# A transformer block on one core: the shared expert computed per 512-token chunk inside the span attention, with routed experts behind it

## The chip, the core and the metric

The kernel runs on one core of a Trainium2 chip. A core has five engines with instruction streams of their own: TensorE (PE: matmuls, with weight loads that overlap them), VectorE (DVE), ScalarE (ACT: activation functions from tables), GpSimd (POOL) and SyncE (SP, which issues most of the transfers). They meet only by semaphores. Matmuls write to eight banks of PSUM (128 partitions x 512 numbers each); everything else lies in SBUF. The metric is the device time of one execution in microseconds.

## What is computed

The reference takes x (32 sequences of 64 tokens, width 256, so 2048 tokens) and a context of 32 x 1601 rows, and applies three residual blocks. Cut to what matters:

```python
x = x + xattn(layernorm(x), ctx, ctx, mask, ...)   # 16 heads of 16, over 1601 keys
x = x + attn(layernorm(x), W_span, W_val, W_out)   # "span attention", below
x = x + ffn(layernorm(x), ...)

# attn: per head, scores depend only on a position and a learned mean and softness
span = head_reshape(h @ W_span.T, 2); value = head_reshape(h @ W_val.T, D)
mean = sigmoid(span[..., 0]) * m; soft = softplus(span[..., 1])
scores = -soft[..., None] * (pos - mean[..., None]) ** 2
out = softmax(scores) @ value; return reshape(out) @ W_out.T

# ffn: one shared expert for all tokens, two routed ones by a hash of the token's number
shared = silu(xf @ sw1 + sb1) * (xf @ sw3 + sb3) @ sw2 + sb2
for k in range(2):                                  # 8 experts, hidden width 256
    ids = (arange(N) * 11 + k * 7919) % 8
    out[tokens of e] += gelu(xs @ w1[e] + b1[e]) @ w2[e] + b2[e]
return (shared + out / 2) / 2
```

The hash depends on the token's number modulo 8 alone, so tokens fall into eight classes of 256, and each class has two experts. The shared expert is 256 to 512 (twice, one with Silu) to 256.

## The kernel before

The kernel works on transposed data: width on the partitions (two tiles, NK = 2), tokens along the columns. It has three phases. The first, cross attention (lines 455 to 842), takes nearly all of the span; the change doesn't touch it. The second and third are built by `tail` (line 845).

**Span attention** (`span_attention`, line 953) runs over four chunks of 512 tokens (eight sequences each). Its order is written out in the kernel, in three strings: `PE_ORDER`, `DVE_ORDER`, `ACT_ORDER`. A letter names a step and the digit its chunk; a repeated step counts its parts. `run_order` emits each engine's steps in that order, each with its semaphore waits. On TensorE: W the output projection of the cross attention, M and V the mean and the variance of the first layer norm (a matmul with a matrix of 1/256), S the span projection, T the transposition of its packed rows, A (eight per chunk) two matmuls that spread a pair of heads' factors, X (four per chunk) the value projections, U the sums of the exponentials, O their products with the values, Z the output projection, and m and v the second layer norm. On ScalarE: Q/q square, I/i inverse root (a logarithm and an exponential), S span activations, T copy of the transposed rows, B copy of a factor, E exponential of the distances, X value copies, L and U logarithm and exponential of the sums. On VectorE: W/Z add to x, C/c centre, N/n normalise, R pack, D distance (a product), O output, F the folding of the expert biases.
Banks 0 and 1 (`proj`) take W and Z, 2 and 3 (`ln_bank`) the layer norms, spans and turned rows, 4 to 7 factors, values, sums and products. All numbers in this part are 32-bit floats; most matmuls take them as two passes, while A and T use a one-pass format (F32R).

**Experts** (`expert_mlps`, line 1282) run after it, over the eight classes of 256 tokens. Every operand is split into a high and a low part in F32R, and `accumulate` (line 1465) makes three matmuls for each product: high-high, low part of the moving side, low part of the weights. Per class and in this order: the two hidden layers of the shared expert (48 matmuls), the first layers of both routed experts (24), and, one class late, the output (24 of the shared and 24 of the routed experts into one bank). ScalarE turns tokens into their high part, applies Silu and Gelu, and casts the results; the functions of the span attention, Silu and Gelu lie in different activation tables, and the program contains a table load at each switch. VectorE makes the low parts, gates, and adds class results to x in place. GpSimd splits the weights as they arrive through two buffers: six pieces early (sw1, sw3 and four first layers), the others once the last chunk's normalised tokens `h2` are complete. The last instruction on SP stores all of x, 2048 KB, after the last result.

Of the kernel before, what the change touches and what calls it, by code (L numbers as in the profile page):

```python
# [22 lines left out]
P = 128  # L23
# [821 lines left out]
def tail(nc, ins, bank, attn_out, out_done, wo, bo_all, mean_w, eps_col, ident, out_dram, sem):  # L845

    with ExitStack() as own:
        def sb(name, shape, dt=F32):
            return own.enter_context(nc.sbuf_tensor(name, shape, dt))

        x = sb("x", [P, NK, NTOK])
        h2 = sb("h2", [P, NK, NTOK])
        wval, wout = (sb(n, [P, NK, D]) for n in ("wval", "wout"))
        wspan = sb("wspan", [P, NK, 2 * H])
        sel_a, sel_b = sb("sel_a", [P, PAIRS, P], F32R), sb("sel_b", [P, PAIRS, P], F32R)
        head_ones = sb("head_ones", [P, 32])

        sw1, sw3 = ([sb(n + part, [P, NK, HS], F32R) for part in ("_hi", "_lo")] for n in ("sw1", "sw3"))
        w1 = [[sb(f"w1_{part}{i}", [P, NK, D], F32R) for part in ("hi", "lo")] for i in range(W_SLOTS)]
        weight = [sb(f"weight{i}", [P, NK * HS]) for i in range(2)]  # L860
        sb1, sb3 = sb("sb1", [P, HS // P]), sb("sb3", [P, HS // P])
        sb2, b1, b2 = sb("sb2", [P, NK]), sb("b1", [P, E, NK]), sb("b2", [P, E, NK])
        class_bias = sb("class_bias", [P, E, NK])
        bias_a, bias_b = sb("bias_a", [P, NK]), sb("bias_b", [P, NK])
        x_in = [sem(f"t_x_in{c}") for c in range(NCH)]
        w_in, sel_in, f_in, y_out = (sem("t_" + n) for n in ("w_in", "sel_in", "f_in", "y_out"))
        h2_done, f_done = sem("t_h2_done"), sem("t_f_done")

        def toks(c):
            return slice(c * CW, (c + 1) * CW)  # L870

        with nc.Block() as block:  # L872
            with ExitStack() as span:
                spans = span_attention(nc, span, bank, sem, mean_w, eps_col, ident, attn_out, out_done, x, h2, wo, bo_all, wspan, wval, wout,
                                       sel_a, sel_b, head_ones, x_in, w_in, sel_in, h2_done)
            mlps = expert_mlps(nc, own, bank, sem, ins, x, h2, weight, sw1, sw3, w1, sb1, sb3, b1, class_bias, f_in, h2_done, f_done, spans["first_rows"])

            @block.sync
            def _(sp):
                def load(tile, src, done):  # L880
                    sp.dma_start(tile, src).then_inc(done, 16)

                def rows(name):
                    return ins[name].rearrange("(k p) n -> p k n", p=P)

                for c in range(2):
                    load(x[:, :, toks(c)], rows("xT")[:, :, toks(c)], x_in[c])
                for name, tile in (("wspanT", wspan), ("wvalT", wval), ("woutT", wout)):
                    load(tile[:], rows(name), w_in)
                load(head_ones[:], ins["c_head_ones"], w_in)  # L890
                for c in range(2, NCH):
                    load(x[:, :, toks(c)], rows("xT")[:, :, toks(c)], x_in[c])
                for name, tile in (("sb1", sb1), ("sb3", sb3), ("sb2", sb2)):
                    load(tile[:], ins[name], f_in)
# [41 lines left out]
            @block.tensor  # L936
            def _(pe):
                spans["tensor"](pe)
                mlps["tensor"](pe)
# [651 lines left out]
```

## Time and profile before

| | us |
|---|---|
| median of 3 runs | 1577.74 |
| lowest, highest | 1574.93, 1578.54 |
| profiled execution | 1581.58 |
| its span | 1579.8 |
| TensorE busy | 1487.5 (94% of the span) |
| VectorE busy | 1002.9 (63%) |
| ScalarE busy | 917.8 (58%) |
| GpSimd busy | 424.8 (27%) |

A span is the profiled execution from its first to its last instruction. Busy time of TensorE includes a modelled way of each result through the array, so short groups of matmuls look longer than the gap to the next start. The granted clock (PEclk) is TensorE's clock as a share of 2.4 GHz; its other level is 1.2 GHz.

### The profile page before, as it was taken

What the parts mean: (1) busy time and instruction counts of PE and PEld (TensorE: products, weight loads), DVE (VectorE), ACT (ScalarE), POOL (GpSimd) and SP (SyncE); (2) the same over time, 40 slices, a digit from 0 to 9 for tenths busy, and PEclk for the clock granted to TensorE, in tenths of its full rate; (3) what the DMA queues carried; (4) which work ended last, traced back from release to release, by engine and by line L of the source; (5) the groups of instructions that cost most, each with busy time, mean ns of one, the idle gap of its engine ahead of it and who ended that gap; (6) DMA issues with size and microseconds to landing.
All of it is one profiled execution on the core that took longest, in us unless ns stands there. A gap on an engine that the chain in (4) does not pass through costs nothing. (4 is left out here: it accounts for less than half of the span.)

```text
span 1579.8 us, 56667 instructions
## 1 busy us (share of the span) xinstructions
PE 1487.5 (94%) x23708; PEld 1264.8 (80%) x23708; DVE 1002.9 (63%) x3974; ACT 917.8 (58%) x1836; POOL 424.8 (27%) x549
## 2 busy tenths in 40 slices
PE   6699999999999999999999999999999978886997
PEld 2578888888888888888888888888888844544997
DVE  4666677677666676767667667766666635442642
ACT  3346666665566665666556666665666644764653
POOL 0033333333333333333333333333333003002420
PEclk9899999999999999999999999999999998998999
DMA  5444444444444444444444444444444222000201
GB/s 150 139 121 109 109 109 109 109 109 109 112 119 121 127 113 106 117 112 121 110 116 114 116 113 117 116 110 110 109 109 109 68 86 85 2 1 8 61 21 54
DMA packets 89856, 156.28 MB, mean 99 GB/s; under 512 B 44784, under 2 KB 53744, under 8 KB 89328
## 3 DMA queue, kind: packets, MB, share of 16 engines
q1 hardware_dynamic: 89312, 151.56, 36.1%
q8 instruction: 191, 3.13, 0.9%
q0 software_dynamic: 288, 1.05, 0.2%
q14 instruction: 65, 0.53, 0.1%
HBM read 69.61 MB, written 4.19 MB: 47 GB/s over the span
## 5 line engine op out<-in xcount | busy, mean ns | idle before, releaser
L663 DVE CUSTOM_DVE_ANT_0 junk<-bank,mask_q 128x400 bf16<-128x400 f32 (+1 forms) x1024 | 546.9, 571 | 186.5 <-issue 180.3
L615 ACT ACTIVATE probs<-bank 128x512 f32<-128x512 f32 (+1 forms) x832 | 467.3, 595 | 123.2 <-PE bank L788 113.9
L591 POOL CAST ctx_hi<-ctx_raw 128x400 fp32r<-128x400 f32 x248 | 121.6, 519 | 847.8 <-PE bank L752 847.8
L788 PE MATMUL bank<-qstack,kstack 104*128 104x128 f16 (+1 forms) x3328 | 290.2, 220 | 4.2 <-ACT probs L615 3.4
L752 PE MATMUL bank<-wv_hi,ctx_hi 128*128 128x256 f32 (+1 forms) x832 | 280.1, 337 | 0.0
L769 PE MATMUL bank<-kstack,qstack 96*128 96x400 f16 (+1 forms) x1024 | 268.2, 336 | 7.4 <-issue 3.8
L654 DVE SCALAR_TENSOR_TENSOR k_lo<-bank,bk,k_hi 128x400 f16<-128x400 f32 (+1 forms) x256 | 162.2, 634 | 168.0 <-ACT k_hi L625 168.0
L635 ACT ACTIVATE v<-bank 128x256 f32<-128x256 f32 (+1 forms) x416 | 159.2, 383 | 188.5 <-PE bank L752 182.1
L788 PEld LDWEIGHTS bank<-qstack,kstack 104*128 104x128 f16 (+1 forms) x3328 | 214.2, 99 | 65.1 <-issue 16.7
L625 ACT ACTIVATE k_hi<-bank,bk 128x400 f16<-128x400 f32 (+1 forms) x256 | 152.1, 594 | 180.4 <-PE bank L742 172.3
L594 POOL TENSOR_TENSOR ctx_lo<-ctx_raw,ctx_hi 128x400 fp32r<-128x400 f32 x248 | 253.2, 1040 | 0.0
L752 PE MATMUL bank<-wv_lo,ctx_hi 128*128 128x256 f32 (+1 forms) x832 | 233.1, 280 | 0.0
L752 PE MATMUL bank<-wv_hi,ctx_lo 128*128 128x256 f32 (+1 forms) x832 | 232.7, 280 | 0.0
L803 PE MATMUL bank<-probs,v 128*32 128x64 f32 x13312 | 219.3, 220 | 8.1 <-issue 8.1
L803 PEld LDWEIGHTS bank<-probs,v 128*32 128x32 f32 x13312 | 197.4, 110 | 24.0 <-issue 16.4
L742 PE MATMUL bank<-ctx_hi,wk_hi 128*128 128x400 f32 (+1 forms) x512 | 190.4, 372 | 10.5 <-issue 9.7
L742 PE MATMUL bank<-ctx_lo,wk_hi 128*128 128x400 f32 (+1 forms) x512 | 177.4, 346 | 0.7 <-issue 0.7
L742 PE MATMUL bank<-ctx_hi,wk_lo 128*128 128x400 f32 (+1 forms) x512 | 178.0, 348 | 0.0
L752 PEld LDWEIGHTS bank<-wv_hi,ctx_hi 128*128 128x128 f32 (+1 forms) x832 | 154.7, 186 | 4.8
L752 PEld LDWEIGHTS bank<-wv_lo,ctx_hi 128*128 128x128 f32 (+1 forms) x832 | 154.9, 186 | 0.1
L752 PEld LDWEIGHTS bank<-wv_hi,ctx_lo 128*128 128x128 f32 (+1 forms) x832 | 153.3, 184 | 0.0
L769 PEld LDWEIGHTS bank<-kstack,qstack 96*128 96x128 f16 x1024 | 82.1, 98 | 55.7 <-issue 19.7
(169 smaller groups left out, 1727.2 us busy)
## 6 DMA issues: line engine op xcount, KB each, us to landing
ctx_raw<-in_ctxT SPq DMA_DIRECT2D x32, 1602.0 KB, 7.0
kstack<-k_hi SPq DMA_DIRECT2D x512, 100.1 KB, 2.2
kstack<-k_lo SPq DMA_DIRECT2D x256, 100.1 KB, 2.2
weight<-in_w SPq DMA_DIRECT2D x18, 256.0 KB, 2.7
x<-in_xT SPq DMA_DIRECT2D x8, 512.0 KB, 5.9
qstack<-q_parts SPq DMA_DIRECT2D x192, 16.0 KB, 5.6
out_yT<-x SPq DMA_DIRECT2D x1, 2048.0 KB, 6.4
weight<-in_sw SPq DMA_DIRECT2D x3, 512.0 KB, 6.6
```

Of the source, the lines that this page charges most:

```text
L591: nc.gpsimd.tensor_copy(c_hi[:, k, s0:s0 + n], raw[:, k, s0:s0 + n]).then_inc(ctx_hi, 1)
L594: nc.gpsimd.tensor_tensor(c_lo[:, k, s0:s0 + n], raw[:, k, s0:s0 + n], c_hi[:, k, s0:s0 + n].bitcast(F32), ALU.subtract).then_inc(ctx_lo, 1)
L615: nc.scalar.activation(probs[kt % NP][0:m, GROUPS * h:GROUPS * (h + 1), :], st[h][0:m, :], ACT.Exp, scale=DK ** -0.5 / (UP * UP)).then_inc ...
L625: nc.scalar.activation(k_hi[:, t, s0:s0 + n], pj[(b.slot + c) % 2][:, 0:n], ACT.Identity, bias=w["bk"][:, t:t + 1]).then_inc(khi_done, 1)
L635: nc.scalar.activation(heads, pj[(b.slot + NCK + i) % 2][0:m, 0:D].rearrange("s (p e d) -> s p e d", e=2, d=DK), ACT.Copy).then_inc(v_done, 1)
L654: nc.vector.scalar_tensor_tensor(k_lo[:, t, s0:s0 + n], pj[(b.slot + c) % 2][:, 0:n], w["bk"][:, t:t + 1], k_hi[:, t, s0:s0 + n], ALU.add, ...
L663: nc.vector.tensor_tensor_reduce(junk[i % SM][:, 0:n], sm[i % SM][:, 0:n], w["mask_q"][:, s0:s0 + n], 1.0, -3.0e38, ALU.add, ALU.max, part ...
L742: mm = nc.tensor.matmul(o, w[wp][:, k, t * P:(t + 1) * P], cp[:, k, s0:s0 + n], start=i == 0, stop=i == len(terms) - 1)
L752: mm = nc.tensor.matmul(o, cp[:, k, j * P:j * P + m], w[wp][:, k, :], start=i == 0, stop=i == len(terms) - 1)
L769: nc.tensor.matmul(sm[i % SM][:, 0:n], qstack[b.slot][0:KSTACK, p, :], kstack[b.slot][0:KSTACK, p, s0:s0 + n], start=True, stop=True).then ...
L788: mm = nc.tensor.matmul(st[h][0:m, g * PW:(g + 1) * PW], kstack[b.slot][0:KROWS, p, kt * P:kt * P + m], qstack[b.slot][0:KROWS, p, :], sta ...
L803: mm = nc.tensor.matmul(ob[32 * g:32 * g + 32, t * S:(t + 1) * S], v[b.slot][0:m, kt, c0:c0 + 2 * DK], probs[kt % NP][0:m, p, S * e:S * (e ...
```

## The change

`span_attention`, `expert_mlps` and the old `tail` become one function, `tail`, with one set of order strings. The shared expert leaves the classes. After a chunk's second layer norm, its tokens are split (H on ScalarE, h on VectorE) and laid out by class in `tokens`, which now holds all 2048; the normalised tokens are written over `xc[1]` and `h2` is gone. The shared expert then works on the 512 tokens of that chunk: F, in four parts (12 matmuls of 512 columns each, into banks 0 and 1; Silu F, gate F, cast G and remainder G behind it), and G, its output (24 matmuls), added to x by VectorE's step r. sw2 is scaled by 0.5 and the sum added directly, where it was scaled by 2 and the joint bank by 0.25. `proj_free` makes each user of banks 0 and 1 wait for all users ahead of it. F and G of chunks 0 to 2 stand between the steps of the span attention of the following chunk, those of chunk 3 between the first routed experts.
The routed experts keep their classes: K, first layers (24 matmuls of 256 columns, in banks 4 and 5 or 6 and 7 by turns), and P, second layers (24, in banks 2 and 3 by turns). Results go to eight tiles `y`, and SP stores each class in a transfer of 256 KB; all of its loads are issued ahead of the first store. The early pieces on GpSimd are now seven: sw1, sw3, sw2 and four first layers, which lie beside the span attention's buffers, while the slots of the second layers reuse them. The exponentials lie in the space of `attn_out`, and the output of the span attention overwrites `rs`. ScalarE's return to the logarithm and exponential table is written as a load by name.

```diff
-    PE_ORDER = """W0 M0 W1 V0 W2 S0 W3 T0 A0 M1 A0 A0 A0 A0 V1 A0 A0 S1 A0 T1 X0 U0 X0 M2 A1 X0 X0 V2 O0 S2 A1 Z0 A1 T2 A1 M3 m0 A1 A1
-        V3 A1 v0 A1 X1 X1 U1 X1 X1 A2 S3 O1 T3 A2 Z1 A2 A2 m1 A2 A2 A2 A2 v1 X2 X2 U2 X2 X2 A3 O2 A3 Z2 A3 A3 m2 A3 A3 A3 A3
-        v2 X3 X3 U3 X3 X3 O3 Z3 m3 v3"""
+    PE_ORDER = """W0 M0 W1 V0 W2 S0 W3 T0 A0 M1 A0 A0 A0 A0 V1 A0 A0 S1 A0 T1 X0 U0 X0 M2 A1 X0 X0 V2 O0 S2 A1 Z0 A1 T2 A1 m0 A1 M3 A1
+        v0 A1 V3 A1 X1 U1 X1 F0 A2 X1 X1 F0 S3 O1 F0 A2 A2 T3 Z1 A2 A2 F0 A2 m1 A2 A2 v1 G0 U2 X2 F1 A3 X2 X2 F1 X2 F1 O2 F1
+        A3 A3 Z2 A3 A3 m2 A3 G1 A3 v2 A3 X3 X3 U3 X3 F2 X3 F2 O3 F2 Z3 m3 F2 v3 G2 K0 F3 K1 F3 K2 F3 P0 F3 K3 P1 K4 G3 K5 K6
+        P2 P3 P4 K7 P5 P6 P7"""
...
+            def log_exp():
+
+                if table[0] != "log_exp":
+                    nc.scalar.preload_act_table_set("natural_log_exp_and_others")
+                table[0] = "log_exp"
...
+            def silu(c, m):
+                n = FT * c + m
+                table[0] = "silu"
+                act.wait_ge(s["f1"], n + 1)
+                if c == 0 and m == 0:
+                    act.wait_ge(s["f_in"], 5 * 16)
+
+                need(act, s["gate_lo_done"], n - 1)
+                nc.scalar.activation(gate[m % 2][:], proj[0][:, :], ACT.Silu, bias=sb1[:, m:m + 1]).then_inc(s["silu_done"], 1)
...
+            def proj_free(m):
+
+                need(pe, s["x1_done"], NK * emitted["W"])
+                need(pe, s["x2_done"], NK * emitted["Z"])
+                need(pe, s["silu_done"] if m == 0 else s["gate_done"], emitted["F"])
+                need(pe, s["shared_done"], NK * emitted["G"])
...
+            def shared_hidden(c, m):
+                pe.wait_ge(s["tok_lo_done"], c + 1)
+                pe.wait_ge(s["w_lo_done"], pieces.index("sw3") + 1)
+                for j, (weights, done) in enumerate(((sw1, s["f1"]), (sw3, s["f3"]))):
+                    proj_free(j)
+                    out = proj[j][:, :].rearrange("p (e t) -> p e t", e=E)
+                    accumulate(out, [(columns(weights, k, m), [chunk_tokens(part, k, c) for part in range(2)])
+                                     for k in range(NK)]).then_inc(done, 1)
+                emitted["F"] += 1
+
+            def shared_output(c, _):
+                pe.wait_ge(s["w_lo_done"], pieces.index("sw2") + 1)
+                pe.wait_ge(s["gate_lo_done"], FT * (c + 1))
+                for m in range(NK):
+                    proj_free(m)
+                    accumulate(proj[m][:, :], [(columns(sw2, k, m), [part[:, k, :] for part in gate_parts])
+                                               for k in range(FT)]).then_inc(s["shared"], 1)
+                emitted["G"] += 1
...
+            def store(n):
+                sp.wait_ge(s["f_done"], NK * (n + 1))
+                dst = out_dram.rearrange("(k p) (e t) -> p k e t", p=P, e=E)[:, :, order[n], :]
+                sp.dma_start(dst, y[n][:]).then_inc(y_out, 16)
```

How the instructions stand on the engines that the prediction walks through. TensorE at the turn from chunk 1 to chunk 2, before; from the top the value projections (L1251), the sums (L1259), a pair A (L1240, L1241), the spans of chunk 3 (L1213), products (L1268), transposition (L1222) and output projection (L1177):

```order
L1251 MATMUL bank<-wval,t_h 128x256 x4
L1259 MATMUL bank<-ex,head_ones 32x512 x8
L1251 MATMUL bank<-wval,t_h 128x256 x4
L1240 MATMUL bank<-rows,sel_a 128x512
L1241 MATMUL bank<-rows,sel_b 128x512
L1213 MATMUL bank<-wspan,t_h 128x32 x8
L1268 MATMUL bank<-ex,vbd 32x64 x64
```

The same place now; L1470 is the helper of the three-pass matmuls, L1445 the value projections, L1453 the sums (the exponentials lie in attn_out), L1434 and L1435 a pair A:

```order
L1445 MATMUL bank<-wval,t_h 128x256 x2
L1453 MATMUL bank<-attn_out,head_ones 32x512 x8
L1445 MATMUL bank<-wval,t_h 128x256 x2
L1470 MATMUL bank<-tokens_hi,sw_hi 128x512
L1470 MATMUL bank<-tokens_lo,sw_hi 128x512
L1470 MATMUL bank<-tokens_hi,sw_lo 128x512
...
L1434 MATMUL bank<-rows,sel_a 128x512
L1435 MATMUL bank<-rows,sel_b 128x512
L1445 MATMUL bank<-wval,t_h 128x256 x4
L1470 MATMUL bank<-tokens_hi,sw_hi 128x512
```

Two parts of F0, twelve matmuls each, stand among the value projections, and only one value projection stands ahead of the sums where two did.

ScalarE at the same place, before: an exponential, value copies (L1069), logarithm and exponential of the sums (L1078, L1083), a factor copy (L1050), and the span activations (L1032 and behind it):

```order
L1059 ACTIVATE ex<-dist 128x512
L1069 ACTIVATE vbd<-bank 64x8x16 x8
L1078 ACTIVATE rs<-bank 128x512 x2
L1069 ACTIVATE vbd<-bank 64x8x16 x4
L1083 ACTIVATE rs<-rs 128x1024
L1069 ACTIVATE vbd<-bank 64x8x16 x4
L1050 ACTIVATE b_copy<-bank 128x512
L1032 ACTIVATE e<-bank 128x64
```

And now, from the token cast (L1165) over the value copies (L1143), Silu (L1176) and gate cast (L1182) to the return of the table (L1079) ahead of the span activations:

```order
L1165 ACTIVATE tokens_hi<-t_xc 128x8x64 x2
L1143 ACTIVATE vbd<-bank 64x8x16 x4
L1153 ACTIVATE rs<-bank 128x512 x2
L1143 ACTIVATE vbd<-bank 64x8x16 x4
L1159 ACTIVATE rs<-rs 128x1024
L1176 ACT_TABLE_LOAD
L1176 ACTIVATE gate<-bank,sb 128x512
L1120 ACTIVATE b_copy<-bank 128x512
L1143 ACTIVATE vbd<-bank 64x8x16 x4
L1182 ACTIVATE gate_hi<-gate 128x512
L1143 ACTIVATE vbd<-bank 64x8x16 x4
L1176 ACTIVATE gate<-bank,sb 128x512
```

Token cast, Silu, gate cast and the switches of tables are new among the span attention's copies and exponentials.

## Rows read from the trace of the kernel before

**Rows 1.** The page's first line: the span and its instructions.

```profile
span 1579.8 us, 56667 instructions
```

**Rows 2.** Windows: start:end, length, then busy us of each engine, PEclk, DMA.

```profile
1372.20:1454.30 82.10, 60.55 (x580) 34.74 (x581) 31.69 (x56) 48.37 (x111) 1.79 (x1) 0.93 0.00 1
1454.30:1572.60 118.30, 116.87 (x960) 116.50 (x960) 55.25 (x94) 63.92 (x108) 34.02 (x31) 0.99 0.10 30
...
1374.10:1400.90 26.80, 23.26 (x213) 14.54 (x212) 13.89 (x28) 18.95 (x44) 0.00 (x0) 0.94 0.01 2
1400.90:1425.70 24.80, 19.33 (x196) 10.91 (x195) 10.19 (x17) 17.36 (x38) 0.00 (x0) 1.00 0.00 1
1425.70:1454.30 28.60, 16.06 (x169) 7.86 (x169) 6.72 (x12) 10.20 (x26) 1.79 (x1) 0.87 0.00 1
```

**Rows 3.** Chain that ended last: start us, length us, engine and line.

```profile
1452.45 0.73 ACT tokens_hi L1380 x2
...
1453.21 0.97 DVE tokens_lo L1419 x2
...
1454.31 110.90 PE bank L1465 x912
...
1566.14 5.99 PE bank L1465 x48
...
1572.16 0.42 DVE x L1441
```

**Rows 4.** Timeline of TensorE: start, length, form, count, [idle before <-releaser].

```profile
1365.65 0.40 PE L1240 MATMUL bank<-rows,sel_a 128*128 128x512 f32 x1
1365.88 0.39 PE L1241 MATMUL bank<-rows,sel_b 128*128 128x512 f32 x1
...
1374.13 1.92 PE L1259 MATMUL bank<-ex,head_ones 128*32 128x512 f32 x16
...
1400.95 1.93 PE L1259 MATMUL bank<-ex,head_ones 128*32 128x512 f32 x16
...
1407.46 1.99 PE L1268 MATMUL bank<-ex,vbd 128*32 128x64 f32 x128 [2.20 <-ACT vbd L1069]
...
1411.48 3.60 PE L1177 MATMUL bank<-o,wout 128*128 128x512 f32 x8
...
1421.59 1.88 PE L1204 MATMUL bank<-t_sq,mean_w 128*128 128x512 f32 x4
...
1425.68 1.92 PE L1259 MATMUL bank<-ex,head_ones 128*32 128x512 f32 x16
1427.54 1.99 PE L1251 MATMUL bank<-wval,t_h 128*128 128x256 f32 x8
...
1436.26 5.63 PE L1177 MATMUL bank<-o,wout 128*128 128x512 f32 x8 [1.44 <-DVE o L1161]
```

**Rows 5.** Groups by line, 1372.2 to 1454.3: busy us, mean ns of one, idle before.

```profile
L1153 DVE TENSOR_TENSOR dist<-bank,b_copy 128x512 f32<-128x512 f32 x16 | 10.6, 686 | 14.5 <-ACT b_copy L1050 12.7 <-ACT ex L1059 1.8
...
L1050 ACT ACTIVATE b_copy<-bank 128x512 f32<-128x512 f32 x16 | 9.1, 596 | 7.3 <-PE bank L1241 7.3
```

**Rows 6.** Timeline of ScalarE in the expert stage, as rows 4.

```profile
1468.61 1.28 ACT L1392 ACT_TABLE_LOAD   x1
1469.91 1.57 ACT L1392 ACTIVATE gate<-bank,sb 128x256 f32<-128x256 f32 x4
```

**Rows 7.** Groups by line on GpSimd, 1290 to 1580, as rows 5.

```profile
L1370 POOL TENSOR_TENSOR w_lo<-weight,w_hi 128x512 fp32r<-128x512 f32 x18 | 24.8, 1378 | 1.4
L1367 POOL CAST w_hi<-weight 128x512 fp32r<-128x512 f32 x18 | 13.0, 723 | 50.9 <-PE bank L1465 47.4 <-DMA weight<-in_w 3.4
...
L1364 POOL TENSOR_SCALAR weight<-weight 128x1024 f32<-128x1024 f32 x1 | 2.8, 2779 | 118.7 <-DVE h L1126 118.7
```

**Rows 8.** DMA issues of the page: KB each, median us from issue to landing.

```profile
weight<-in_w SPq DMA_DIRECT2D x18, 256.0 KB, 2.7
...
out_yT<-x SPq DMA_DIRECT2D x1, 2048.0 KB, 6.4
```

More of the change, by code:

```diff
@@ L963, in span_attention @@
     BLOCKS = CW // P
-    xc = [sb(f"t_xc{i}", [P, NK, CW]) for i in range(2)]
-    sq = [sb(f"t_sq{i}", [P, NK, CW]) for i in range(2)]
-    rstd = [sb(f"t_rstd{i}", [P, CW]) for i in range(2)]
-    h = [sb(f"t_h{i}", [P, NK, CW]) for i in range(2)]
-    e0, lnx, near, gap = (sb(n, [P, BLOCKS, H]) for n in ("e0", "lnx", "near", "gap"))
-    sg = sb("soft_gap", [P, BLOCKS, 2 * H])
-    packed = sb("packed", [P, BLOCKS, P], F32R)
-    ident_r = sb("ident_r", [P, P], F32R)
-    rows = [sb(f"rows{i}", [P, CW], F32R) for i in range(2)]
@@ L1308, in expert_mlps @@
+    assert max(i for i, step in enumerate(PE_ORDER.split()) if step[0] == "W") < min(PE_ORDER.split().index(step) for step in ("Z0", "F0"))
     order, arrival = [0], list(CLASS_EXPERTS[0])
@@ L1520, in expert_mlps @@
-    return {"sync": sync, "gpsimd": gpsimd, "scalar": scalar, "vector": vector, "tensor": tensor}
+    pieces += [("w1", i) for i in range(W_SLOTS)]
+    NEARLY = len(pieces)
+    pieces += [("w2", 0), ("w2", 1)] + [(w, i + lag) for i in range(E + 1 - W_SLOTS) for w, lag in (("w2", 2), ("w1", W_SLOTS))]
+    pieces += [("w2", i) for i in range(E + 3 - W_SLOTS, E + 1)]
+    names = ("x1_proj x1_done x2_proj x2_done span e0_done lnx_abs lnx_exp lnx_done vec packed_zero vbd_zero turn_ready packed_done turned "
+             "rows_done ab_ready b_copied dist_done ex_done sums lns_done rs_done val_ready vbd_done pv o2_done h_done h2_done "
+             "tok_hi_done tok_lo_done f1 f3 silu_done gate_done gate_hi_done gate_lo_done shared shared_done fe gelu_done gelu_hi_done "
+             "gelu_lo_done xb_done f_out f_done w_halved w_hi_done w_lo_done w_in sel_in f_in").split()
@@ new lines, in tail @@
+    s = {n: sem("t_" + n) for n in names}
+    x_in = [sem(f"t_x_in{c}") for c in range(NCH)]
+    weight_in = [sem(f"t_weight_in{i}") for i in range(2)]
+    y_out = sem("t_y_out")
+    mean, xc_done, sq_done, var, lnv, rstd_done = ([sem(f"t_{n}{i}") for i in range(2)]
+                                                   for n in ("mean", "xc", "sq", "var", "lnv", "rstd"))
+    norm_done = [s["h_done"], s["h2_done"]]
+    src_done = [s["x1_done"], s["x2_done"]]
+    bias_steps = sem("t_bias_steps")
```

973 lines of the change are left out of this document (478 added, 495 removed).

## Prediction

> **What bounds the kernel now.** I read the windows first, because an average over the whole span mixes stages. The attention over the context ends near 1291 us and the diff leaves it alone. Behind it lie the span attention (to 1454.3) and the expert stage. In the expert stage TensorE is busy 116.87 of 118.3 us; before it, from 1372.2 to 1454.3, 60.55 of 82.1 us, at a mean clock of 0.93, with ScalarE at 48.37 and VectorE at 31.69 [rows 2]. The chain of waits says the same: its last long piece is 110.90 us of matmuls on line 1465, then 5.99 us more, one result of 0.42 us, and the store [rows 3]. So the second stage is bound by TensorE's work, and the first by waits among three engines, in which TensorE stands still. Work carried from the second into the holes of the first can be had for less than its length. The question is how full the holes get.
>
> The first stage repeats per chunk. I take the matmuls of "sums" (the sums of the exponentials, line 1259) as milestones: U1 starts at 1374.13, U2 at 1400.95, U3 at 1425.68 [rows 4]. The last piece, U3 to the first expert matmul at 1454.31, is a bare dependency chain: 16.06 us busy of 28.6 [rows 2, 3].
>
> **Prices.** An expert matmul of 256 columns: 912 of them in 110.90 us [rows 3], 0.1216 each; with the first ones at half clock out of it 0.120. One of 512 columns in the same number format: two start 0.23 apart [rows 4], and that pair also changes its weights; twice 0.107 of streaming is 0.213. I take 0.22, within 0.213 and 0.23. The shared expert has 24 x 3 = 72 such matmuls per chunk: F, four pieces of 12 (2.6 us each, 10.5 together), and G, 24 (5.3). That is 15.8 per chunk, 63.4 in all; as 576 narrow ones it cost 69.1. The routed experts stay: 384 x 0.12 = 46.1.
> ScalarE gains per chunk four Silus, four casts and two token casts of 512 columns, near 0.60 each by the b_copy row [rows 5] (two token casts of half the width take 0.73 [rows 3]), so 6.0. A table switch occupies 1.28 [rows 6]. The order of the new kernel has 6 switches with chunk 0's pieces, 4 with chunk 1's, 2 with chunk 2's and 9 in the routed stage, 21 behind the first against 16 before. VectorE gains four gates, four remainders, two token remainders and two additions, 12 x 0.69 [rows 5] = 8.2 us per chunk; the class-permuted ones are bounded by 0.69 and by 0.97, the two narrow remainders of [rows 3]. It was busy 10.19 of 24.8 in the second cycle [rows 2]; VectorE does not bind.
>
> **Floors per cycle.** Second cycle: TensorE 19.33 busy at full clock [rows 2] plus 15.8 is 35.1. ScalarE 17.36 plus 6.0 plus 4 x 1.28 is 28.5. First cycle, ScalarE: 18.95 + 6.0 + 6 x 1.28 = 32.6. So TensorE remains the bound, with ScalarE close behind, and a new cycle cannot take less than about 35 where the old took 24.8 or 26.8.
>
> **Walking the new order.** I followed the three orders by hand, each step starting when its engine is free and what it reads is there, with these prices: on TensorE an averaging or variance step 1.8, an output projection 3.5, X 0.97, U 1.9, O 2.0, a pair A 0.46 (all issue time, by [rows 4], where the printed length holds also the last matmul's way through the array); on ScalarE 0.55 to 0.60 for 512 columns; on VectorE 0.69, 1.3 for a pair.
> U1: variance v0 now stands ahead of V3, so the last distance of chunk 1 comes earlier; U1 at 1372.3, 1.8 early (between 0 and 2). The first F waits for the token remainder until 1375.2.
> U1 to U2: U1 ends at 1374.2, X follows, F runs from 1375.2 to 1377.8. Its first half lets ScalarE begin at 1376.5, but there stand two groups of value copies, the sums' logarithm and their exponential; so the switch is at 1377.7, the Silu 1379.0 to 1379.6, the gate ends 1380.4. TensorE has A and two X until 1380.2: the second F waits for nothing. S, O and the third F end at 1389.3. T3 needs the packed rows, which VectorE makes from 1388.1 on, behind O1's outputs: 1390.7. Z1 runs 1391.3 to 1394.9; the last F waits for Z1's addition (1396.4) and ends at 1399.0; m1 at 1399.5; v1 waits for the square, which stands behind a Silu, a cast and two copies (1404.1); G0 1406.0 to 1411.2; U2 at 1411.2. TensorE's work in it is 35.6, so 3.3 idle.
> U2 to U3: Z2 waits for the switch and the fourth Silu (1431.2), G1 runs 1438.5 to 1443.7 over the squares, X3 waits for the last distance (1448.0); U3 at 1450.0, 36.1 of work and 2.7 idle.
> U3 to the routed experts: F2 pieces wait for Silu, switch and gate; Z3 at 1465.6, m3 1470.6, v3 1475.0, G2 1477.7 to 1482.9 over the inverse root, switch, normalisation, cast and remainder of chunk 3; routed experts at 1483.6, with 28.5 of work and 5.1 idle.
> Sum: 1372.3 + 100.2 work + 11.1 idle = 1483.6. Of the 100.2, 3 x 15.8 = 47.4 is carried in; the old kernel took 80.2 for the other 53 and stood or ran slowly for 27. So 47 us of work come in and the stage ends 29.3 later: 18 hidden.
> From there TensorE has 46.1 of routed work and 15.8 of chunk 3's shared work, 61.9. It should not wait: banks are double and results alternate; ScalarE has 9 switches (11.5), four Silus, four casts and the first three classes' activations against about 35 us up to the last G. The weight splits that now come behind the phase are 14, at 0.72 + 1.38 = 2.1 [rows 7], 29 in all; the first output needs two (4.2) and starts 16 us in. They hide; uncovered, the first two would cost 4.2. Doubling sw2 took 2.8 on GpSimd [rows 7]; its halving moves into the idle time before 1372, at nothing, since the first G is at 1406. The eight bias additions of x, now behind chunk 3's shared addition, cost VectorE some 5 us before the third result while TensorE has 2.8 per class: 0 to 2, I take 0.5. End of matmuls 1483.6 + 61.9 + 0.5 = 1546.0.
> **The end.** Result 0.4. The old store took from 1572.58 to 1579.8, 7.2, of it 6.4 landing for 2048 KB; a 256 KB load lands in 2.7 [rows 3, 8]. With the same 0.8 around it the last of eight stores takes 3.5, bounds 2.7 (nothing around it) and 7.2. That makes 1549.9.
> **Clock.** In the old stage Z3 took 5.63 against 3.60 for Z2, behind a wait of 1.44 [rows 4]; the granted clock of that cycle was 0.87 against 1.00 in the one before [rows 2], so part of it at 1.2 GHz. The walk has full clock. The new holes are shorter; I add 2, between 0 and 5 (what the old run lost). Span 1552; minus 27.8 against 1579.8 [rows 1]. The profiled execution took 1581.58, 1.8 above its span, and the median of the runs is 1577.74, so the change goes off that: **1549.9**.
>
> **Rivals.**
> *Holes filled wholly.* Neither idle nor slow clock: 1372.3 + 100.2 + about 3, then 61.9 and 3.9: 1541 span, 1539 predicted. For it: an order that keeps independent work at every wait. Against: F needs both output banks, which the residual path also uses.
> *Nothing hidden.* The waits stay as long and the shared work adds itself: 1372.3 + 53 + 27 + 47.4 + 61.9 + 3.9 = 1565.5, so 1563.4. Still faster, by narrow matmuls made wide (5.7), the smaller last store (3.7), and the early U1, wait and slow clock at the old seam. For it: ScalarE at 32.6 of the first cycle's 38.9, and each of 12 switches can stand ahead of an exponential for which X waits.
> *Switches dearer than their rows.* In the old trace a switch follows the cast at once and the next activation starts 1.30 behind it [rows 6]. If instead each cost its 1.28 once more on the path, the 12 of the span stage would add 15.4 to the span of 1552 (1565 predicted), and all 21 would add 26.9 (1577). The Trainium skill, ScalarE: Activation LUTs, section "What ACT_TABLE_LOAD costs", gives 1283 ns for the load and 1380 ns of drain, 2.66 us a switch. By that rule the 12 add 16.6 and the 21 add 29, so 1566.5 and 1579; the trace agrees with its 1283 but shows no second part.
> *Slower: pieces run one behind another.* F writes the two banks that Z writes. If every piece ran alone (2.6 matmul, 1.28 switch, 0.60 Silu, 0.69 gate = 5.2, four of them, then cast, remainder, 5.3, addition and switch back, 9.3) a chunk would cost 30, three 90: experts at 1372.3 + 80.2 + 90 = 1542.5, span 1608, predicted 1606. It decides from 20.5 us a chunk, against 15.8 of matmul. Against it: between F pieces stand A, X, S and O, which use other banks.
> *It doesn't do what it says:* the routed stage waits for weights. Fourteen splits each with its load unhidden, 2.1 + 2.7 = 4.8, are 67 against 61.9: 5 more, 1555; inside the forecast's range.
>
> **Chances.** Forecast (1543 to 1557) 0.60; filled wholly 0.13; nothing hidden or a part of the dearer switches (1557 to 1570) 0.19; dearer switches in full, about no change, 0.02; slower 0.06. A measurement can tell 0.2% from no change, some 3 us. Faster 0.92, same 0.02, slower 0.06. The range takes half of the outer two cases and the bounds of clock and store: 1538 to 1567.
>
> **What would show it.** In the profile after: U2 near 1411, U3 near 1450, first routed matmul near 1484 (right within 5); F matmuls 0.22 apart; TensorE waits in the routed stage under 2 us; switches 1.28; last store about 3.5. TensorE waiting for Silus or distances over 20 us between 1372 and the routed start would make the walk wrong; a routed stretch over 66 would make its hidden switches or weights wrong; a routed start later than 1514 would make it slower.

## The result, and the profile after

The changed kernel takes 1549.88 us (median of 4 runs, 1546.79 to 1550.99) against 1577.34 for the kernel before (4 runs, 1574.93 to 1578.54): 27.5 us less, ratio 0.9825, interval 0.9806 to 0.9844. The profiled execution took 1546.79 with a span of 1545.0.

The span is 34.8 us shorter than that of before, but not all of this is the change. The output projection W0, the first matmuls that the diff touches, starts at 1284.47 where it started at 1292.25: 7.8 us lie in the attention ahead of it, which is the same code; in the profiles of the variants below, with this same attention, it starts anywhere from 1281.2 to 1291.1. From W0 to the end of the span it is 260.5 us, where it was 287.5. That is 27.0 less, close to the difference of the medians. The steps are therefore compared below by their distance from W0.

Windows of the changed kernel: start:end, length, busy us of each engine, PEclk (the granted clock), DMA share, GB/s. The cuts are W0, the milestones U1, U2 and U3, the first routed matmul, and the last one's end.

```profile
core 0: us, PE busy (x) PEld busy (x) DVE busy (x) ACT busy (x) POOL busy (x), PEclk, DMA share, GB/s
1284.50:1363.40 78.90, 66.65 (x337) 36.37 (x337) 46.55 (x94) 40.82 (x83) 21.80 (x17) 0.88 0.28 88
1363.40:1403.10 39.70, 37.37 (x283) 26.10 (x282) 21.72 (x40) 33.32 (x61) 0.00 (x0) 1.00 0.00 1
1403.10:1443.20 40.10, 37.56 (x273) 25.91 (x272) 18.24 (x28) 28.76 (x53) 0.00 (x0) 1.00 0.01 2
1443.20:1478.30 35.10, 30.57 (x241) 19.75 (x240) 13.34 (x20) 19.16 (x35) 0.00 (x0) 1.00 0.00 1
1478.30:1541.70 63.40, 62.90 (x458) 59.13 (x456) 33.44 (x60) 37.17 (x65) 30.42 (x28) 1.00 0.26 80
```

These rows answer to [rows 2]. The two cycles grew from 26.8 and 24.7 to 39.7 and 40.1, and in them TensorE is now busy 94% of the time, at full clock, where it was busy 23.26 of 26.8 and 19.33 of 24.8. The stage of expert matmuls shrank from 118.3 to 63.4. The whole path from U1 (1363.39) to the first routed matmul (1478.45) is 115.1; before it was 80.2 to the first expert matmul, so 34.9 longer, for 216 matmuls of the shared expert carried in.

What still stops TensorE between 1362 and the end, from its waits (line waited, releaser, us in total, times, longest):

```profile
PE bank L1445 <- DVE dist L1291: 3.1, 2, 1.7
PE bank L1392 <- DVE x L1243: 1.8, 2, 1.4
PE bank L1363 <- DVE gate L1311: 1.7, 2, 1.0
PE bank L1434 <- DVE dist L1291: 1.5, 1, 1.5
PE bank L1470 <- ACT gate L1176: 1.3, 1, 1.3
PE bank L1470 <- issue: 1.2, 2, 0.8
PE bank L1470 <- DVE x L1243: 0.7, 1, 0.7
```

In all 11.3 us. Of the first line, 1.7 stands just ahead of U1, so 9.6 lie between U1 and the end: 2.9 for distances, 3.0 for gates and a Silu, 2.5 for additions to x, and 1.2 that the view puts down to no engine. The end of the chain that ended last, which answers to [rows 3] (start, length, what):

```profile
1471.89 0.82 issue
1472.71 53.92 PE bank L1470 x360
1526.63 0.39 issue
1527.02 14.59 PE bank L1470 x120
1541.63 0.42 DVE y L1344
1542.06 0.33 DVEq L1529
```

From 1472.71 TensorE runs its 480 last matmuls with one stop of 0.39: no weight, Silu or Gelu is waited for. From the last result (1542.06) to the end of the span is 2.9 us.

### The profile page after: what moved, and what is told of

Its sections match the earlier page's. It is cut to its first block and busy times, and to the rows that moved or that the text cites. A ratio compares the mean times of both kernels' runs of the same rounds, so it can differ in the third digit from the quotient of the medians.

```text
span 1545.0 us, 56243 instructions
## 1 busy us (share of the span) xinstructions
PE 1473.8 (95%) x23420; PEld 1243.0 (80%) x23420; DVE 1007.9 (65%) x3974; ACT 926.2 (60%) x1833; POOL 426.2 (28%) x549
## 3 DMA queue, kind: packets, MB, share of 16 engines
q0 software_dynamic: 288, 1.05, 0.2%
```

## The experiments

Times are medians; "before" is the kernel before on the same chip. Only the edit against the changed kernel is shown.

### The shared expert behind the span attention, in the new and in the old order

`e1_shared_behind` takes F and G of chunks 0 to 2, with their casts, gates and additions, out of the three strings and sets them behind the span attention.

```diff
...
-        v0 A1 V3 A1 X1 U1 X1 F0 A2 X1 X1 F0 S3 O1 F0 A2 A2 T3 Z1 A2 A2 F0 A2 m1 A2 A2 v1 G0 U2 X2 F1 A3 X2 X2 F1 X2 F1 O2 F1
-        A3 A3 Z2 A3 A3 m2 A3 G1 A3 v2 A3 X3 X3 U3 X3 F2 X3 F2 O3 F2 Z3 m3 F2 v3 G2 K0 F3 K1 F3 K2 F3 P0 F3 K3 P1 K4 G3 K5 K6
+        v0 A1 V3 A1 X1 U1 X1 A2 X1 X1 S3 O1 A2 A2 T3 Z1 A2 A2 A2 m1 A2 A2 v1 U2 X2 A3 X2 X2 X2 O2 A3 A3 Z2 A3 A3 m2 A3 A3 v2
+        A3 X3 X3 U3 X3 X3 O3 Z3 m3 v3 F0 F0 F0 F0 G0 F1 F1 F1 F1 G1 F2 F2 F2 F2 G2 K0 F3 K1 F3 K2 F3 P0 F3 K3 P1 K4 G3 K5 K6
...
```

> The changed kernel with F, G and r of chunks 0 to 2 moved out of the span attention, to between its last step and the first routed expert (11 table loads in place of 22). Theory, that the shared work fills holes of the span attention: 47 us of TensorE work no longer hidden, against 11 us of idle that stay in the changed kernel and 27 in the old cycles, so 16 longer, plus up to 3 us of bank and gate waits per chunk where nothing else stands between the pieces: +14 to +25 on 1549.9, 1564 to 1575. Rival, that the gain came from wide matmuls and the small store alone: the order doesn't matter, within +3.

Measured: 1587.03 against 1577.29, ratio 1.0064 (1.0041 to 1.0086): 0.6% above the kernel before, and 37 above the changed one, outside what was expected. Its window from U1 to U2, and in the timeline the output projection Z1 in it:

```profile
1366.40:1401.50 35.10, 25.64 (x209) 15.24 (x208) 14.68 (x29) 19.69 (x45) 0.00 (x0) 0.85 0.00 1
...
1383.79 6.39 PE L1363 MATMUL bank<-rs,wout 128*128 128x512 f32 x8
```

Without its pieces this cycle still takes 35.1, with 9.5 us of it idle and the clock at 0.85.

`e5_old_order` does the same to the span attention's steps in the order of the kernel before.

```diff
...
-        v0 A1 V3 A1 X1 U1 X1 F0 A2 X1 X1 F0 S3 O1 F0 A2 A2 T3 Z1 A2 A2 F0 A2 m1 A2 A2 v1 G0 U2 X2 F1 A3 X2 X2 F1 X2 F1 O2 F1
...
+        V3 A1 v0 A1 X1 X1 U1 X1 X1 A2 S3 O1 T3 A2 Z1 A2 A2 m1 A2 A2 A2 A2 v1 X2 X2 U2 X2 X2 A3 O2 A3 Z2 A3 A3 m2 A3 A3 A3 A3
+        v2 X3 X3 U3 X3 X3 O3 Z3 m3 v3 F0 F0 F0 F0 G0 F1 F1 F1 F1 G1 F2 F2 F2 F2 G2 K0 F3 K1 F3 K2 F3 P0 F3 K3 P1 K4 G3 K5 K6
...
```

> The changed kernel with the order strings of the kernel before for the span attention (the token casts and remainders H and h added right behind each chunk's second layer norm), and F, G, r of chunks 0 to 2 behind it, as in e1. It parts the price of not interleaving from that of running the new order with its pieces taken out. In e1 the cycles U1 to U2 and U2 to U3 took 35.1 and 29.0 us where the kernel before took 26.8 and 24.7, and the shared chunks behind took 20.4 each. Theory, that the new order leans on its pieces (and the clock on the work): the cycles are back near 27 and 25 and the time near 1577 (1573 to 1581). Rival, that token casts or the merged function slow the cycles whatever the order: 1585 to 1589 as e1.

Measured: 1585.07 against 1575.53, ratio 1.0051 (1.0029 to 1.0074). That is outside the 1573 to 1581 of the theory and on the rival's figure: the cycles are shorter than in e1, but not back at 27 and 25, and the whole is no faster than e1 against its kernel before. Its windows, cut at U1, U2, U3, the second piece of F0 and the first routed matmul:

```profile
1371.70:1401.70 30.00, 24.11 (x213) 13.65 (x212) 15.00 (x30) 19.90 (x45) 0.00 (x0) 0.94 0.00 1
1401.70:1429.50 27.80, 21.28 (x193) 12.15 (x192) 11.34 (x19) 18.56 (x40) 0.00 (x0) 0.94 0.00 1
1429.50:1462.50 33.00, 20.30 (x182) 11.08 (x181) 8.18 (x14) 12.89 (x28) 0.68 (x2) 0.84 0.00 1
1462.50:1521.40 58.90, 50.31 (x204) 39.20 (x205) 20.95 (x29) 16.25 (x24) 5.83 (x5) 0.97 0.05 14
```

And a piece of its chain that ended last, from the switch ahead of the first Silu to the second chunk (start, length, what):

```profile
1460.37 1.28 ACT L1176
...
1461.66 0.70 ACT gate L1176
...
1462.49 8.61 PE bank L1470 x36
1471.11 2.28 issue
1473.38 7.40 PE bank L1470 x24
...
1480.81 0.70 DVE x L1325
...
1481.64 11.38 PE bank L1470 x48
```

This settles why the work carried in is worth more than the windows of before and after suggest. Here the path from U1 to the first routed matmul takes 149.7 us; in the changed kernel 115.1. Against this placement, putting the pieces inside therefore saves 34.7, not the 15.4 of a net comparison (50.3 of matmuls, 34.9 more path). The other 19 (149.7 less 80.2 less 50.3) are costs that the shared expert per chunk brings by itself when it stands behind, and that the holes swallow too. A better order behind the span attention, with the next chunk's F over the last one's chain, was not run; the 34.7 holds against e5's. The two cycles are 3.2 and 3.1 longer than in [rows 2]. In them ScalarE now also casts tokens (19.90 busy for 18.95, 18.56 for 17.36), and the clock fell to 0.94 in the second; how the 3 us part between these two is not shown. The third stretch holds one F piece and is 1.6 longer beyond that; in it TensorE waits 3.27 for the switch and the first Silu. The last has 58.9 for 204 matmuls that take 47.5 at 0.233: between the last F piece and G stands a chain of gate, cast and remainder, 2.28 for each of three chunks, at the first two G's end 0.9 passes until the next F, and G0 took 7.40 where the next took 5.86, part of it at the low clock.

Of the change as a whole: all of it but the placing costs 8 to 10 (ratio 1.0051, by its interval 5 to 12; the medians differ by 9.5), and the placing gives back 35.

### The shared expert of chunks 0 to 2 left out

`e4_no_shared_012` is e1 without those steps at all (on all three engines; semaphore counts start at chunk 3), so that their 216 matmuls are not done.

```diff
-                n = FT * c + m
+                n = FT * (c - 3) + m
...
-                pe.wait_ge(s["gate_lo_done"], FT * (c + 1))
+                pe.wait_ge(s["gate_lo_done"], FT * (c - 2))
```

> The changed kernel without the shared expert of chunks 0 to 2 (F, G and r left out for them; chunk 3 keeps it). Measures what 47.4 us of TensorE work cost where they stand. Theory (18 of 47 hidden): 28 to 33 faster, 1517 to 1522. Rival, nothing hidden: 47 faster or more, 1503. Rival, hidden wholly: 20 faster.

Measured: 1530.12 against 1577.29, ratio 0.9686 (0.9654 to 0.9719): 19.8 below the changed kernel. The theory wanted 28 to 33, and 20 is the figure of the rival that says "hidden wholly". But the number flatters: the order without its pieces slows itself. Three of TensorE's waits between U1 and the end:

```profile
PE bank L1467 <- DVE tokens_lo L1300: 5.3, 1, 5.3
PE bank L1459 <- ACT vbd L1140: 4.6, 2, 3.3
...
PE bank L1450 <- ACT attn_out L1130: 2.5, 1, 2.5
```

The first two have their like in the kernel before (4.6 ahead of the first expert matmul, 4.9 for value copies); the third, for an exponential, has none there. The cycles show the slowing: they take 34.9 and 32.1, at clocks of 0.85 and 0.89, where the old order with the same token casts takes 30.0 and 27.8 (e5). An order written around inserted work has that work's holes in it, so taking the work out doesn't measure what it costs.

### The pieces one behind another

`e9_serial_pieces` lets TensorE wait behind each F piece until its gate is made, so that nothing stands between the matmuls and the gate.

```diff
                 emitted["F"] += 1
+                pe.wait_ge(s["gate_done"], emitted["F"])
```

> The changed kernel with a wait of TensorE behind each of the 16 pieces F for the gate of that same piece, so that nothing stands beside a piece's switch, Silu and gate. Rival of the prediction, that the pieces run one behind another and make the kernel slower than before, decides from 28 us over 1549.9. A piece's Silu may follow its first half; where ScalarE is free and no switch is due, 0.9 remains behind the piece, with a switch or older copies ahead of it 2 to 4: 16 x 0.9 to 16 x 3, so +14 to +48, 1564 to 1598, likeliest near 1580. Theory that other work hides all of it in the changed kernel needs this to be clearly over +10.

Measured: 1575.08 against 1577.78, ratio 0.9976 (0.9960 to 0.9991), 22 above the changed kernel as measured beside it (`e11_same`), 25 above its first median, and inside what was expected. U1 to U2 takes 48.2, U2 to U3 46.6. The largest of TensorE's waits:

```profile
PE bank L1434 <- DVE gate L1311: 8.8, 5, 2.4
PE bank L1445 <- DVE gate L1311: 3.6, 2, 2.8
PE bank L1470 <- DVE gate L1311: 3.5, 4, 1.0
```

Nearly all of the gain against before is gone with a placing that only lets go of the gate. This is the rival "one behind another", made real for F. From U1 to the first routed matmul it is 134.3, 54.1 more than before the change, and the routed stage, in which four pieces wait too, takes 67.7 for 63.2. Together that is 58.6, or 19.5 a chunk; the prediction named 20.5 a chunk as the point from which the change loses, and the ratio is indeed just below one. What keeps the changed kernel off that point is that A, X, S and O stand between the F pieces.

### Table switches, doubled and taken away

`e2_double_switch` loads another table first wherever one is loaded.

```diff
                 if table[0] != "log_exp":
+                    nc.scalar.preload_act_table_set("exp_and_others")
                     nc.scalar.preload_act_table_set("natural_log_exp_and_others")
...
+                if table[0] != "silu":
+                    nc.scalar.preload_act_table_set("natural_log_exp_and_others")
                 table[0] = "silu"
...
             def gelus(n, j):
+                if table[0] != "gelu":
+                    nc.scalar.preload_act_table_set("natural_log_exp_and_others")
+                table[0] = "gelu"
```

> The changed kernel with every one of the 21 table loads behind the first done twice (43 loads in place of 22), 1.28 us more of ScalarE each. Theory, switches mostly off the path, but ScalarE near full in the cycle with chunk 0's pieces (33.3 busy of 39.7): six more there are 7.7 and spill by some 3 to 6, the other fifteen by 1 to 5 together: +4 to +11. Rival, that each switch lies on the path: +27, 1577. Rival, that they are all covered: under +2.

`e3_no_switch` uses the exponential in place of Silu and Gelu.

```diff
-                nc.scalar.activation(gate[m % 2][:], proj[0][:, :], ACT.Silu, bias=sb1[:, m:m + 1]).then_inc(s["silu_done"], 1)
+                nc.scalar.activation(gate[m % 2][:], proj[0][:, :], ACT.Exp, bias=sb1[:, m:m + 1]).then_inc(s["silu_done"], 1)
```

> The changed kernel with Exp in place of Silu and Gelu, so that no table is switched (1 load; the activation functions are other ones, their shapes the same). Theory: TensorE is 94 percent busy in the cycles and waits 11 us in all, of which gates and distances behind switches are a part: 2 to 5 faster, 1545 to 1548. Rival, that 12 or 21 loads lie on the path: 15 to 27 faster.

Measured: doubled 1573.64 (ratio 0.9975, 0.9960 to 0.9990), taken away 1549.05 (0.9818, 0.9792 to 0.9845), both against 1577.29. Taking all but one away gives 0.8, within the noise and less than the 2 to 5 expected; adding as many costs 23.8, far above the 4 to 11 expected and near the 27 of the rival that has each one on the path. The profiles tell it without the noise of the attention ahead: from U1 to the first routed matmul it is 113.0 without switches, 115.1 with them (115.0 to 115.1 in four further profiles of this order) and 128.5 doubled; the routed stage takes 63.0, 63.2 and 69.3. So the 21 switches cost about 2 us, and 21 more cost 19.5 in these stretches. Doubled, the windows of the two cycles and the two largest waits of TensorE are these:

```profile
1369.40:1414.40 45.00, 39.24 (x285) 26.70 (x287) 20.47 (x38) 40.87 (x67) 0.00 (x0) 0.96 0.00 1
1414.40:1460.10 45.70, 39.61 (x273) 26.41 (x272) 19.48 (x30) 33.77 (x57) 0.00 (x0) 0.96 0.01 1
```

```profile
PE bank L1476 <- ACT gate L1179: 7.5, 5, 2.6
PE bank L1369 <- DVE gate L1317: 6.5, 3, 3.3
```

The order has room for one switch at each place and for hardly any of a second, so no single price per switch describes it. The expectation (4 to 11) took ScalarE's busy share for its room; but the second switch lands ahead of a Silu or an exponential that the next group of matmuls waits for, and in the first cycle ScalarE is then busy 40.87 of 45.0.

### Wide matmuls, stores, weights

`e6_narrow` issues each shared product in two halves of 256 columns, `e7_one_store` stores all classes at once behind the last result, `e8_late_routed` splits the four first layers only behind the span attention.

```diff
...
-                    accumulate(proj[m][:, :], [(columns(sw2, k, m), [part[:, k, :] for part in gate_parts])
-                                               for k in range(FT)]).then_inc(s["shared"], 1)
+                    for half in range(2):
+                        cs = slice(half * CW // 2, (half + 1) * CW // 2)
+                        i = accumulate(proj[m][:, cs], [(columns(sw2, k, m), [part[:, k, cs] for part in gate_parts])
+                                                        for k in range(FT)])
+                    i.then_inc(s["shared"], 1)
```

```diff
...
-            for n in range(E):
-                store(n)
-            sp.wait_ge(y_out, 16 * E)
+            store()
+            sp.wait_ge(y_out, 16)
```

```diff
-    pieces += [("w1", i) for i in range(W_SLOTS)]
     NEARLY = len(pieces)
+    pieces += [("w1", i) for i in range(W_SLOTS)]
```

> The changed kernel with every shared matmul of 512 columns made as two of 256 (576 for 288, same steps and waits). By the measured starts, 0.233 apart for 512 and 0.120 for 256: 576 x 0.120 less 288 x 0.233 is 2.0, so 1 to 3 longer. Rival, the term of the prediction (0.220 for 512): 5.7 longer.

> The changed kernel with one result tile and one store of 2048 KB behind the last result. The end behind the last result, 3.0 us in the changed kernel's profile, goes back to about 7.2: 3.7 to 4.5 longer in the profile's end, about 1554. Rival, that the store of eight parts brings nothing (stores queue behind late loads on SP): under 1.

> The changed kernel with the four early first-layer weights split after the span attention, with the rest, not before. The first routed expert then waits for two splits (2.1 each) behind the last chunk's tokens, and the later ones queue behind two more: 4 to 8 longer. Rival, that GpSimd has room and the early slots bring nothing: under 1.

All against 1575.53:

| | median | ratio (interval) | above 1549.88 |
|---|---|---|---|
| e6_narrow | 1551.59 | 0.9843 (0.9821 to 0.9865) | 1.7 |
| e7_one_store | 1554.76 | 0.9876 (0.9850 to 0.9901) | 4.9 |
| e8_late_routed | 1555.18 | 0.9874 (0.9849 to 0.9900) | 5.3 |

The last column compares medians taken apart; the changed kernel itself, measured again in `e11_same`, lay 2.8 above its first median.

Narrow: a piece F takes 2.84 where the wide one takes 2.80. Two starts of 512 columns are 0.233 apart and two of 256 are 0.120, so a wide matmul saves 3% by these and 1% by the whole piece, not the 8% that 0.22 would give. From U1 to the end the profile is 1.1 longer; the medians of 1.7 agree with that and don't exclude zero. One store: the chain of e7 and, behind it, the transfer in its page:

```profile
1544.71 0.33 DVEq L1528
...
out_yT<-y_all SPq DMA_DIRECT2D x1, 2048.0 KB, 6.5
```

From there to the end of its span (1551.9) it is 7.2, as before the change [rows 1, 3], and 2.9 with eight stores. Late routed weights, from the waits of e8:

```profile
PE bank L1470 <- POOL w_lo L1071: 3.9, 1, 3.9
```

The one new wait stands between G2 and K0 (it ends at 1483.91), and no class behind it waits for weights. But the stage behind it takes 65.9, where it takes 63.2 in the changed kernel, and the granted clock of its first 16.1 us is 0.81, where it is 1.00 there. So the early routed weights are worth the wait once, and 2.8 more of slow matmuls behind it. From U1 to the end of the span that is 6.8 by the two profiles; the medians, taken apart, differ by 5.3.

### Matmuls that only keep TensorE busy

In the changed kernel TensorE stands still for 4.70 us ahead of W0 and runs W0 slowly. `e10_warm_seam` adds 18 matmuls behind the last attention products whose results nobody reads; `e12_warm_chunk0` adds to these 7 and 16 in two holes of the stage of chunk 0. `e11_same` is the changed kernel again.

```diff
             products(at(B - 1), KT - 1)
+            pe.wait_ge(v_done, KT * B)
+            for i in range(18):
+                nc.tensor.matmul(pj[0][:, 0:400], w["wk_hi"][:, 0, 0:P], c_hi[:, 0, 0:400], start=True, stop=True)
```

```diff
-    PE_ORDER = """W0 M0 W1 V0 W2 S0 W3 T0 A0 M1 A0 A0 A0 A0 V1 A0 A0 S1 A0 T1 X0 U0 X0 M2 A1 X0 X0 V2 O0 S2 A1 Z0 A1 T2 A1 m0 A1 M3 A1
+    PE_ORDER = """W0 M0 W1 V0 W2 S0 W3 T0 A0 M1 A0 A0 A0 A0 V1 A0 A0 d0 S1 A0 d1 T1 X0 U0 X0 M2 A1 X0 X0 V2 O0 S2 A1 Z0 A1 T2 A1 m0 A1
...
+            def dummies(c, _):
+                pe.wait_ge(s["x1_done"], NK * NCH)
+                for i in range((7, 16)[c]):
+                    nc.tensor.matmul(proj[0][:, :], sel_a[:, 0, :], sel_a[:, 0:4, :], start=True, stop=True)
```

> The changed kernel with 18 further matmuls of 400 columns behind the last products of the cross attention (their result isn't used), in the wait ahead of W0, to see whether W0 then runs at full clock. W0 takes 5.96 us in the changed kernel's profile and 3.60 at full clock. If what TensorE did just before matters: W0 near 3.6 to 4.6 and the time 1 to 2.4 shorter. Rival: the clock falls anyway in the 2 us of the block's end: W0 unchanged, time the same.

> The changed kernel unchanged, for a comparison with e10 on the same chip: 1548 to 1552; the stretch from W0 to U1, 78.9 us in its first profile, anywhere from 78 to 83 (80 to 82 in the variants with the same order there), since the granted clock differs there from run to run.

> e10 with further unused matmuls in two holes of chunk 0: 7 of 512 columns ahead of S1 (a wait of 1.7 us) and 16 ahead of T1 (a wait of 4.3 to 6.0 us), in a bank that is free there. U0 took 3.19 us in the changed kernel and 2.48 in e10, and 1.9 at full clock. If the fall of the clock behind holes costs time there: S1 1.97, U0 1.9, the stretch from W0 to U1 77 or less against 77.8 in e10 and 78.9 and 80.3 in the changed kernel, and the time 0 to 2 under 1548. If the chain through ScalarE and VectorE sets that stretch alone: U0 near 1.9 but the time as e10, 1546 to 1550.

Measured: e10 1548.38 (ratio 0.9809, 0.9785 to 0.9832) and e11 1552.71 (0.9829, 0.9805 to 0.9853) against 1577.78; e12 1549.68 against 1575.96 (0.9822, 0.9799 to 0.9845). TensorE's timeline ahead of W0 in e10 and, below it, in the changed kernel:

```profile
1281.06 3.56 PE L836 MATMUL bank<-ctx_hi,wk_hi 128*128 128x400 f32 x18
1285.97 3.67 PE L1366 MATMUL bank<-attn_out,wo 128*128 128x512 f32 x8 [1.35 <-PEq L155]
```

```profile
1284.47 5.96 PE L1363 MATMUL bank<-attn_out,wo 128*128 128x512 f32 x8 [4.70 <-PEq L155]
```

W0 takes 3.67 for eight matmuls where it took 5.96, and 5.08 in e11: the mechanism is there. Its worth is not settled. In the profiles of e10 and e12, U1 comes 77.8 and 78.1 behind W0; in nine with the same steps up to there and no added matmuls it comes 78.9 to 83.4. e10 is 4.3 below its neighbour e11, but 1.5 below the first median of the same kernel, and the intervals overlap; all that can be said is that it is no slower. e12's own matmuls brought nothing on top: S1 ran at full clock (1.97 where the changed kernel has 3.30, but 1.97 in e10 too), and TensorE still waited 2.54 for the packed rows behind the added matmuls. From S1's start to the transposition T1 it is 8.58 in the changed kernel, 8.55 in e10, 8.71 in e11 and 8.70 in e12: that chain lies on ScalarE and VectorE, and TensorE's clock doesn't matter to it. No run that does all of the work beats the changed kernel by more than its interval.

## Why the prediction was right, step by step

Distances from W0; predicted ones are those of the walk less 1292.25, where W0 started in the trace it was made from.

| | predicted | measured |
|---|---|---|
| U1 | 80.1 | 78.9 |
| U2 | 119.0 | 118.6 |
| U3 | 157.8 | 158.7 |
| first routed matmul | 191.4 | 194.0 |
| end of matmuls | 253.8 | 257.1 |
| clock, result and store | 2 + 0.4 + 3.5 | 0.4 + 2.9 |
| end of span | 259.8 | 260.5 |

**U1**, 1.1 too late: the early V and v0 are worth 3.0 here, taken as 1.8. But nine profiles with the same steps up to there place U1 from 78.9 to 83.4 behind W0, 81.1 on average, and the old order has 81.9 in the kernel before and 82.7 in e5; the 1.8 is neither shown nor refuted.

**The cycles**, 38.9 and 38.8 predicted, 39.7 and 40.1 measured, and from U3 to the routed experts 33.6 predicted, 35.2 measured. The idle time of the walk was right in size: 11.1 up to the routed experts, against 9.2 in nine waits of the view above. (The view counts idle time from the printed end of a matmul, the walk from the moment when the next could have started. For a wide matmul these lie 0.40 less 0.23, so 0.17 apart, and nine times that makes it an estimated 10.7.) Its places were right for the distances, Z behind a gate, F behind a Silu and Z's addition; the waits of v1 and v3 for their squares didn't come. Most of the missing microseconds are in the price of the wide matmul.

**The term that was mis-sized** is "I take 0.22, within 0.213 and 0.23". The rows of one piece after the change (starts in the first column):

```profile
1367.37 0.39 PE L1470 MATMUL bank<-tokens_hi,sw_lo 128*128 128x512 f32 x1
1367.60 0.40 PE L1470 MATMUL bank<-tokens_hi,sw_hi 128*128 128x512 f32 x1
1367.83 0.40 PE L1470 MATMUL bank<-tokens_lo,sw_hi 128*128 128x512 f32 x1
```

0.23 apart, and twelve take 2.80 in the chain that ended last: 0.233. The pair A of [rows 4] showed exactly this, and I went below it on the ground that the pair changes its weights; so do these, two times in three. It is 0.0133 x 288 = 3.8 us, 2.9 up to the first routed matmul and 1.0 behind it, of the 4.5 by which the way from U1 to the end of the matmuls was longer than predicted (178.2 for 173.7). The rest, 0.9 of the 3.8 ahead of the routed experts, is not parted here. The gain by width, predicted as 5.7, is therefore 1 to 2 (e6).

**The clock term** of +2 was not needed: PEclk is 1.00 in all stretches from U1 on, and Z1, Z2 and Z3 take 3.67 each, where Z3 took 5.63 in [rows 4]. e1 and e4 show the link: with the pieces taken out of the holes the same steps run at 0.85, and Z1 takes 6.39. So the pieces do not only fill holes, they also keep the clock up for what stands around them. That this error of 2 too much, U1's 1.1 and the store's 0.6 cancel the 4.5 too little of the matmuls is luck; the agreement of the medians to 0.1 is no measure of the walk.

**Switches.** The rival "dearer than their rows" falls, by e3 (2 us for all switches on the path) and by the trace. ScalarE at the turn from Gelu to Silu:

```profile
1482.41 1.28 ACT L1176 ACT_TABLE_LOAD   x1
1483.71 0.69 ACT L1176 ACTIVATE gate<-bank,sb 128x512 f32<-128x512 f32 x1
```

The Silu starts 1.30 behind the load, as in [rows 6]. The Trainium skill, ScalarE: Activation LUTs, section "What ACT_TABLE_LOAD costs", has 1.38 us of drain on top of the 1.28; the trace agrees with the load and shows no drain. What e2 adds: that they are nearly free depends on room for about as many as there are.

**Weights and the routed stage** were hidden, as taken: 63.2 (1478.45 to 1541.6) against 61.9 and 0.5, with 1.0 of the difference in wide matmuls and 0.39 in one stop; the 0.5 for the bias additions was not needed.

**The store** was 2.9 against 3.5 (between 2.7 and 7.2); e7 gives its worth as 4.3 in the profile and 4.9 in the medians, where 3.7 was predicted.

**"Nothing hidden" was priced wrongly**, though it was not the case that came. It said 1563.4; with the work behind instead of inside, e5 measured 1585 and e1 1587, above the kernel before. Its sum kept the old waits as they were and added matmuls. It left out the chain of gates (2.28 a chunk), the first switch, the longer cycles and the slow clock, 19 us together, and 3 for the wide matmuls. The chances of faster, 0.92, rested on that rival being faster as well; they were too sure. What separated this change from a small loss was the placing: e5, with the rest of the change and without it, is 0.5% slower than the kernel before.

## What to carry to other kernels

Where one stage waits on chains and the next is bound by one engine, move independent pieces of the second into the holes of the first, but price the moved work as it would stand alone, with its own chains, before calling the rest hidden: here the placing was worth 35 us and everything else together cost 8 to 10. Test such an order by adding as well as by removing: removing the switches or the pieces said little, doubling the switches showed that the room was nearly used up. Price a new shape by the nearest row and not by the streaming rate: 0.233 was in the trace.

## What the runs showed of the hardware

**GpSimd's weight splits hold up VectorE.** In chunk 0 the packed rows come late. VectorE and, below it, GpSimd of the changed kernel (start, length):

```profile
1326.55 1.37 DVE L1284 TENSOR_TENSOR packed<-soft_gap,packed 128x128 fp32r<-128x128 f32 x1
...
1328.63 1.13 DVE L1230 TENSOR_TENSOR bias_b<-b 128x2 f32<-128x2 f32 x1
1329.80 0.16 DVE L1231 SCALAR_TENSOR_TENSOR class_bias<-bias_b,bias_a 128x2 f32<-128x2 f32 x1
```

```profile
1326.52 1.26 POOL L1071 TENSOR_TENSOR w_lo<-weight,w_hi 128x512 fp32r<-128x512 f32 x1
...
1328.47 1.27 POOL L1071 TENSOR_TENSOR w_lo<-weight,w_hi 128x512 fp32r<-128x512 f32 x1
```

An addition of two columns takes 1.13, where the next of its kind takes 0.16, and ends at 1329.76, with GpSimd's remainder at 1329.74; the first ends at 1327.92, GpSimd's at 1327.78. The 128x128 one took 0.29 before the change, where GpSimd was idle; there another operation of the same chain took 1.05 and ended within 0.1 of GpSimd's remainder. In e10 three operations of this chain take 1.38, 1.27 and 1.38, 4.0 us of the 8.55 from S1 to T1. The run `e8_late_routed` takes the four routed splits out of this place and leaves the rest alone. GpSimd is idle there from 1322.6 on, and VectorE has:

```profile
1325.00 0.29 DVE L1284 TENSOR_TENSOR packed<-soft_gap,packed 128x128 fp32r<-128x128 f32 x1
...
1326.01 0.16 DVE L1230 TENSOR_TENSOR bias_b<-b 128x2 f32<-128x2 f32 x1
```

The nine operations that make the packed rows take 2.3 us in all, where they take 4.7 in the changed kernel and 6.1 in e11, and from S1 to T1 it is 6.29, where the twelve other profiles of the new function have 8.5 to 9.1. So the splits are the cause. Not every operation is held up: the distances of chunk 0, which read a bank, keep their 0.69 beside the splits of the shared weights. Nor does the gain reach U1: in e8 it comes 80.7 behind W0, inside the range of the others. Splitting these weights somewhat later, behind this chain but ahead of the routed experts, was not run.

**Idle time ahead of matmuls costs twice.** W0 behind 4.70 of idleness takes 5.96 and behind the added matmuls 3.67; Z1 takes 3.67 among the pieces and 6.39 without them; and the routed stage of e8, behind its wait of 3.9, runs 2.8 longer than without it.
